# A fused two-layer kernel on one core: the mixer's skip term and its running sums are moved off GpSimd, and the residual is added ahead of y

## The chip, the cores and the metric

The kernel runs as one program on one core of a Trainium2 chip. The metric is the device time of one execution in microseconds, lower is better. A core has five engines with instruction streams of their own, which wait for each other only through semaphores: PE (TensorE, matrix products), DVE (VectorE), ACT (ScalarE), POOL (GpSimd) and SP (SyncE, which issues the DMAs).

## The reference

Two layers are applied to x (1024 tokens, 512 wide): a Mamba-2 style mixer, a SwiGLU block with 4-bit weights, a small attention and a LoRA mixture. Only the mixer is touched:

```
proj = layernorm(x) @ in_proj_w.T              # gate | hbc | dt
xBC  = silu(conv4(hbc) + conv_bias)            # x | B | C ; 64 heads of 64, 8 groups, state 128
state_t = state_{t-1} * exp(dt A) + (dt x)_t B_t ;  y_t = state_t C_t
y   = y + x * D
yn  = y * rsqrt(mean over the group's 512 columns of y*y + eps) * norm_weight * silu(gate)
x   = x + yn @ out_proj_w.T
```

## The kernel before, in words

The mixer is one pipeline over 8 groups of heads (8 heads, 512 columns each) and, inside a group, over 8 chunks of 128 tokens: 64 chunks, n = 8 g + c. Groups 1 to 6 are a hardware loop; group 0 and the last one are written out. Each engine has a fixed program order; semaphores are counted up by the engine named in their prefix. I call the chunks of a group c0 to c7.

In a chunk PE does, in this order: transposes of x into `p_x`; the products of B and C (`p_gb`); the decay exponents (L1081 into `p_in`, L1090 into the two banks `p_d0`, `p_d1`; both read as p_d in the trace); one convolution tile of the next half group (`conv_tile` "now", bank `p_tile`, three passes, L94 and L98); the output product of the chunk before (`out_product(n-1, p_d0)`, also L94 and L98, tile p_d); the state's contribution to y (L1113, `p_in`); the new state (L1121, `p_x`); in c0, c1, c4, c5 a second convolution tile ("later", bank `p_gate`); `sum_rows(n-1)`, a product with a column of ones that sums the squares of y (L1029, a column of `p_gb`); the chunk's own y (L1136, `p_y`); and a tile of gate projections (`next_gate`). `p_d0` thus holds first the decay exponents of chunk n, which ACT reads as the first em, and then the output product of chunk n-1, which DVE adds into the residual stream x_res (`residual`, L742). The decay product of chunk n+1 therefore waits for `s_res`.

DVE does the causal mask (L814), a copy of B (L815), the convolution taps (`tile_taps`: L714 over 509 to 511 columns from PSUM; L722 over 3 to 1 columns at the seam of two halves, from the SBUF tile halo), the masking of em (L826), y = p_in * e_cum (L838), the state update (L844), y += p_y (L856), the gate multiplication (L864), `residual` and `z_rest` (L734). ACT takes the exponentials (L626 em, L628 e_cum), the bias and last tap (L592), SiLU (L597, L613), the squares of y (L650), and rounds z and the weights (L602, L581, L584). POOL scales x by dt (L492, L495), decays the state (L483, `state_dec`), makes D times x (L498, `x_d`) and adds it to y (L515), folds the squares to 128 columns (L525, L528), splits weights (`w_rest` L543; `out_rest`, L551 and L554, two of the output weights in c0) and takes the power -1/2 of the variance (`norm`, L538), which `residual` needs.

The order that matters below is DVE's at the end of a chunk: y, gate multiplication, `residual`, `z_rest`; then ACT's squares, z, gate SiLU, the copy xs, a table load, em.

## Time and profile before

| | us |
|---|---|
| median of 3 runs | 1321.4 (1320.72 to 1321.72) |
| the profiled execution, its time | 1320.9 |
| its span, first to last instruction | 1319.1 |
| mixer's chunks, about | 62 to 986 of the span |
| one group of the loop | 116.4 |

PE is busy 93% of the span, DVE 72%, POOL 54%, ACT 53%. Busy PE time is the modelled end of each product, so that a product that had to wait shows as idle time ahead of its first instruction. The rows of the trace stand in a section below.

### The profile page before, as it was taken

To read this page: it belongs to the slowest core of one execution; us is meant where nothing else is said; L and a number is where in the kernel's file an instruction comes from. 1 tells how busy PE (TensorE), PEld (TensorE's weight loads), DVE (VectorE), ACT (ScalarE), POOL (GpSimd) and SP (SyncE) were. 2 spreads that over 40 slices of the span, in tenths; PEclk is the share of its full clock that TensorE was granted. 3 is DMA by queue.
4 is the path that set the end of the run, shared out by engine and by line. 5 is a ranking of instruction groups with operands and counts; after the bars stand their busy time and mean duration, and the time that the engine had idled before them with its cause. 6 is when DMAs were issued, how large, how long until landed. Compare 5 with 4: busy or idle time off the path is not lost.

```text
span 1319.1 us, 22013 instructions
## 1 busy us (share of the span) xinstructions
PE 1227.4 (93%) x6690; PEld 973.3 (74%) x6690; DVE 953.9 (72%) x1718; ACT 694.1 (53%) x1042; POOL 709.0 (54%) x739
## 2 busy tenths in 40 slices
PE   5999999999999999999999999999779999889986
PEld 4778877887777778777777877778557777667764
DVE  5786768678676866777687677769776555569995
ACT  3666675576667656665766667666333333222220
POOL 5066666666656665675566567555663444343330
PEclk9999999999999999999999999999889999999996
DMA  5111021011102101110110110010003223121200
GB/s 175 46 49 34 1 66 33 18 33 48 33 1 63 34 17 33 48 33 1 48 49 17 33 48 25 9 38 2 20 27 110 95 88 97 47 92 33 59 16 25
DMA packets 44233, 57.52 MB, mean 44 GB/s; under 512 B 10117, under 2 KB 21159, under 8 KB 43929
## 3 DMA queue, kind: packets, MB, share of 16 engines
q1 hardware_dynamic: 44185, 56.92, 14.6%
q8 instruction: 25, 0.41, 0.1%
q14 instruction: 23, 0.19, 0.1%
HBM read 49.95 MB, written 6.96 MB: 43 GB/s over the span
## 4 chain that ended last, share of the span: by engine, by line
PE 57%; DVE 19%; issue 9%; POOL 7%; ACT 5%; DMA 1%; DVEq 1%; SPq 1%; POOLq 0%; ACTq 0%
PE p_tile L94 9%; PE p_d L94 6%; DVE conv L714 6%; PE p_gate L94 5%; PE p_tile L98 4%; PE p_d L98 3%; PE p_y L1136 3%; DVE conv L722 3%; PE p_gate L98 2%; PE p_in L1113 2%; PE t_p_a L1886 2%; POOL y L515 2%; PE p_x L1121 2%; PE p_y L94 2%; PE p_d L1090 2%
## 5 line engine op out<-in xcount | busy, mean ns | idle before, releaser
L714 DVE SCALAR_TENSOR_TENSOR conv<-p_tile,conv_taps,conv 128x511 f32<-128x511 f32 x189 | 141.4, 748 | 49.2 <-ACT conv L592 34.1
L515 POOL TENSOR_TENSOR y<-y,x_d 128x512 f32<-128x512 f32 x56 | 72.2, 1288 | 129.8 <-DVE y L838 129.8
L826 DVE TENSOR_TENSOR em<-em,p_gb 128x512 f32<-128x512 f32 x128 | 82.1, 682 | 53.6 <-ACT em L626 53.5
L714 DVE SCALAR_TENSOR_TENSOR conv<-p_gate,conv_taps,conv 128x511 f32<-128x511 f32 (+2 forms) x90 | 66.9, 743 | 66.9 <-ACT conv L592 66.0
L597 ACT ACTIVATE xbc<-conv 128x512 f32<-128x512 f32 x96 | 60.7, 633 | 101.0 <-DVE conv L722 78.7
L94 PE MATMUL p_tile<-xn_hi,wc_hi 128*128 128x512 f32 x252 | 107.7, 427 | 2.3 <-ACT gate_second L613 1.4
L650 ACT ACTIVATE squares<-y 128x512 f32<-128x512 f32 x64 | 40.6, 634 | 121.1 <-DVE y L856 114.1
L94 PE MATMUL p_d<-wr_hi,zt_hi 128*128 128x512 f32 x252 | 102.5, 407 | 0.8 <-ACT em L626 0.8
L94 PE MATMUL p_d<-wr_lo,zt_hi 128*128 128x512 f32 x252 | 101.8, 404 | 0.0
L94 PE MATMUL p_tile<-xn_lo,wc_hi 128*128 128x512 f32 x252 | 98.6, 391 | 0.0
L492 POOL TENSOR_TENSOR x_w<-xs,head_g 128x512 f32<-128x512 f32 x56 | 61.6, 1101 | 55.3 <-ACT xs L622 50.3
L597 ACT ACT_TABLE_LOAD x61 | 78.3, 1283 | 5.8 <-DVE conv L722 3.2
L626 ACT ACT_TABLE_LOAD x61 | 78.3, 1283 | 1.5 <-PE p_d L1090 0.2
L543 POOL TENSOR_TENSOR wc_lo<-w_raw,wc_hi 128x512 fp32r<-128x512 f32 x48 | 61.2, 1291 | 22.8 <-ACT wc_hi L581 22.8
L626 ACT ACTIVATE em<-p_d 128x512 f32<-128x512 f32 x128 | 69.6, 596 | 5.6 <-PE p_d L1090 5.0
L495 POOL TENSOR_TENSOR x_dt<-xs,head_g 128x512 f32<-128x512 f32 x64 | 67.3, 1052 | 8.1 <-ACT xs L622 8.1
L525 POOL TENSOR_TENSOR squares<-squares 128x256 f32<-128x256 f32 x64 | 62.4, 976 | 16.8 <-ACT squares L650 16.5
L1324 POOL TENSOR_TENSOR f_w_lo<-wf,f_w_hi 128x512 fp32r<-128x512 f32 x22 | 30.4, 1380 | 72.9 <-ACT f_w_hi L1357 72.9
L98 PE MATMUL p_d<-wr_hi,zt_lo 128*128 128x512 f32 x252 | 69.2, 397 | 0.0
L1136 PE MATMUL p_y<-em,x_dt 128*64 128x128 f32 x1008 | 68.9, 279 | 0.0
L498 POOL TENSOR_TENSOR x_d<-xbc,d_g 128x512 f32<-128x512 f32 x64 | 68.2, 1066 | 0.0
L98 PE MATMUL p_tile<-xn_hi,wc_lo 128*128 128x512 f32 x252 | 67.9, 391 | 0.0
(384 smaller groups left out, 3615.3 us busy)
## 6 DMA issues: line engine op xcount, KB each, us to landing
w_raw<-w SPq DMA_DIRECT2D x108, 256.0 KB, 2.7
q_words<-q SPq DMA_DIRECT2D x33, 256.0 KB, 2.6
h_ring<-h_lo_rows SPq DMA_DIRECT2D x6, 704.0 KB, 4.8
h_lo_rows<-h_rest SPq DMA_DIRECT2D x11, 256.0 KB, 2.0
x_res<-x SPq DMA_DIRECT2D x8, 256.0 KB, 4.6
out<-out_t SPq DMA_DIRECT2D x8, 256.0 KB, 2.0
h_lo_rows<-h_rest SPq DMA_DIRECT2D x11, 128.0 KB, 1.9
gate_second<-w SPq DMA_DIRECT2D x4, 256.0 KB, 5.3
```

Source lines behind the costliest of these rows:

```text
L94: pe.matmul(out, lhs(k)[0], rhs(k)[n], start=(start and k == 0 and n == 0), stop=False)
L98: last = pe.matmul(out, lhs(k)[1], rhs(k)[0], start=False, stop=(k == k_tiles - 1))
L492: pool.tensor_tensor(by_head(x_w[:]), by_head(xs[:]), heads(DTW, c), ALU.mult)\
L495: pool.tensor_tensor(by_head(x_dt[:]), by_head(xs[:]), heads(DT, c), ALU.mult)\
L498: pool.tensor_tensor(by_tile(x_d[:]), xbc[:, 0:GW // P, c * P:(c + 1) * P], by_col(d_g[:]), ALU.mult)\
L515: pool.tensor_tensor(y[:], y[:], x_d[:], ALU.add).then_inc(s_txd, 1)
L525: pool.tensor_tensor(squares[:, 0:2 * P], squares[:, 0:2 * P], squares[:, 2 * P:4 * P], ALU.add)\
L597: act.activation(xbc[:, j, half_cols(hf)], conv[:, j % 2, :], ACT.Silu).then_inc(s_xc, 1)
L626: act.activation(em[:, c % 2, k * 512:(k + 1) * 512], p[:], ACT.Exp).then_inc(s_e, 1)
L714: ve.scalar_tensor_tensor(out=conv[:, s, sh:], in0=p[:, 0:HALF - sh], scalar=conv_w[:, bass.ds(g, 1), j, tap], in1=conv[:, s, sh:], op0=AL ...
L826: ve.tensor_tensor(m, m, gm.unsqueeze(1).broadcast_to([P, HG // 2, P]), ALU.mult)\
L1136: mm = pe.matmul(y_bank(last, c)[a:a + HD, j * P:(j + 1) * P], x_dt[:, h * HD:(h + 1) * HD], em[:, c % 2, h * P:(h + 1) * P], start=True, ...
```

## The change

1. D times x: the tile `x_d` and both POOL operations (L498, L515) are gone. DVE adds d_g[j] * xbc[:, j] in four column operations of 128x128, one for each of the 4 tiles of the group: for c > 0 in place in y behind the state update, for c0 with `p_y` as the addend in place of L861. `s_xd` is now DVE's own count.
2. The sum of squares goes into column 384 of y's bank (`p_y`) in place of `p_gb`: PE does `sum_rows(n-1)` right behind `out_product(n-1)`, DVE reads it (`variance`) behind the taps of the "now" tile, and the product L1136 into `p_y` waits for that reading (`s_v`, n).
3. `residual` stands ahead of y's last addition; in c0 DVE's split of two output weights (`w_rest`) goes ahead of it too. POOL's `norm` stands between the two `out_rest` of c0.
4. ACT rounds the four output weights of c0 ahead of that chunk's SiLU; in c0, c1, c4, c5 it takes the gate's SiLU ahead of z's rounding.
5. In the last group's chunks 4 to 7 the output product goes to `p_gate`, with no wait for em, and POOL folds the squares first; rows of the next norm (`row_rest`) go ahead of y's last addition.

The core of the diff:

```
-        return p_gate[:, 0:1] if last and CH <= c < NC else p_gb[:, 3 * P:3 * P + 1]
+        return (p_y if c < NC else p_gb)[:, 3 * P:3 * P + 1]
+    def out_bank(last, c):
+        return p_gate if last and c >= CH else p_d0
...  GpSimd
+                if last and c >= CH:
+                    sum_squares(n - 1)
-                wait(pool, s_y, n)
-                pool.tensor_tensor(by_tile(x_d[:]), xbc[:, 0:GW // P, c * P:(c + 1) * P], by_col(d_g[:]), ALU.mult)\
-                    .then_inc(s_xd, 1)
-                    for w in (OUT + 2, OUT + 3):
-                        out_rest(g, w)
+                    out_rest(g, OUT + 2)
+                if not (isinstance(g, int) and n == 0):
                     norm(n - 1, (c - 1) % 2)
-                    pool.tensor_tensor(y[:], y[:], x_d[:], ALU.add).then_inc(s_txd, 1)
+                if c == 0:
+                    out_rest(g, OUT + 3)
...  ScalarE
+                if c == 0:
+                    wait(act, s_out, n)
+                    for w in ROUNDED:
+                        w_round(g, w)
                 for tile in left + now:
                     tile_silu(*tile)
...
+                made = gate_tile(g, last, c)
+                if made and c % CH < 2:
+                    gate_silu(CH + n, made[1], made[2], gate_bank(c))
                 z_round(n, y_bank(last, c))
...  VectorE
                 for tile in now:
                     tile_taps(*tile, range(TAPPED[tile[3]]))
+                if not first:
+                    variance(n - 1, (c - 1) % 2, ss_bank(c))
...
+                if c > 0:
+                    ve.wait_ge(s_head, 4 * (g + 1))
+                    ve.wait_ge(s_t, st)
+                    for j in range(GW // P):
+                        mm = ve.scalar_tensor_tensor(out=y[:, j * P:(j + 1) * P], in0=xbc[:, j, c * P:(c + 1) * P],
+                                                     scalar=d_g[:, j:j + 1], in1=y[:, j * P:(j + 1) * P],
+                                                     op0=ALU.mult, op1=ALU.add)
+                    mm.then_inc(s_xd, 1)
+                if c == 0:
+                    for w in VE_LO:
+                        w_rest(g, w)
+                if not first and not tail:
+                    residual(n - 1, (c - 1) % NC, out_bank(last, c))
+                for k in rows_in(last, c):
+                    row_rest(k)
...
-                if not first and not tail:
-                    residual(n - 1, (c - 1) % NC)
-                for k in rows_in(last, c):
-                    row_rest(k)
...  TensorE
-                    out_product(n - 1, p_d0)
+                    out_product(n - 1, out_bank(last, c))
+                    sum_rows(n - 1, ss_bank(c))
...
                 pe.wait_ge(s_m, 2 * (n + 1))
-                if not first and not tail:
-                    sum_rows(n - 1, ss_bank(last, c))
...
-                    wait(pe, s_zlo, n)
+                    wait(pe, s_v, n)
```

Where this moves instructions, first on VectorE, chunk c0 of the loop's body. Before, from the state's copy to the two weight splits:

```order
L847 COPY state<-p_x 128x512 [waits pe_inter,ve_stu,pe_stn]
...
L714 SCALAR_TENSOR_TENSOR conv<-p_gate,conv_taps,conv 128x511
...
L729 TENSOR_SCALAR ssv<-p_gb 128x1 [waits pool_rs]
L861 TENSOR_TENSOR y<-x_d,p_y 128x512 [waits act_sq,ve_z,pool_xd,pe_intra]
...
L864 TENSOR_TENSOR p_y<-y,gate_first 128x512 [waits act_sg]
...
L742 SCALAR_TENSOR_TENSOR x_res<-p_d,g_rstd,x_res 128x512 [waits ve_res]
L734 TENSOR_TENSOR zt_lo<-p_y,zt_hi 128x512 [waits act_zhi]
...
L752 SCALAR_TENSOR_TENSOR wr_lo<-w_raw,norm_scale,wr_hi 128x512
```

The same stretch of the change:

```order
L844 COPY state<-p_x 128x512 [waits pe_inter,ve_stu,pe_stn]
...
L748 SCALAR_TENSOR_TENSOR wr_lo<-w_raw,norm_scale,wr_hi 128x512
...
L738 SCALAR_TENSOR_TENSOR x_res<-p_d,g_rstd,x_res 128x512 [waits ve_res]
...
L710 SCALAR_TENSOR_TENSOR conv<-p_gate,conv_taps,conv 128x511
...
L872 SCALAR_TENSOR_TENSOR y<-xbc,d_g,p_y 128x128 [waits ve_head]
L872 SCALAR_TENSOR_TENSOR y<-xbc,d_g,p_y 128x128 x3
...
L880 TENSOR_TENSOR p_y<-y,gate_first 128x512 [waits act_sg]
L730 TENSOR_TENSOR zt_lo<-p_y,zt_hi 128x512 [waits act_zhi]
```

The two splits and the residual now stand between the state and y. Second, VectorE in chunk c1 of the loop's body, before, from the state's part of y on:

```order
L838 TENSOR_TENSOR y<-p_in,e_cum 128x512 [waits ve_z,act_sq,pe_inter]
...
L844 TENSOR_TENSOR state<-p_x,state_dec 128x512 [waits pool_std,ve_stu,pe_stn]
...
L729 TENSOR_SCALAR ssv<-p_gb 128x1 [waits pool_rs,pe_ss]
L856 TENSOR_TENSOR y<-y,p_y 128x512 [waits pool_txd,pe_intra]
L864 TENSOR_TENSOR p_y<-y,gate_first 128x512 [waits act_sg,ve_y]
L742 SCALAR_TENSOR_TENSOR x_res<-p_d,g_rstd,x_res 128x512 [waits ve_res,pool_rs,pe_out]
```

and in the change:

```order
L725 TENSOR_SCALAR ssv<-p_y 128x1 [waits pool_rs,pe_ss]
L835 TENSOR_TENSOR y<-p_in,e_cum 128x512 [waits ve_z,act_sq,pe_inter]
...
L841 TENSOR_TENSOR state<-p_x,state_dec 128x512 [waits pool_std,ve_stu,pe_stn]
L849 SCALAR_TENSOR_TENSOR y<-xbc,d_g,y 128x128 [waits ve_t,ve_head]
L849 SCALAR_TENSOR_TENSOR y<-xbc,d_g,y 128x128 x3
L738 SCALAR_TENSOR_TENSOR x_res<-p_d,g_rstd,x_res 128x512 [waits ve_res,pool_rs,pe_out]
...
L866 TENSOR_TENSOR y<-y,p_y 128x512 [waits pool_xd,pe_intra]
L880 TENSOR_TENSOR p_y<-y,gate_first 128x512 [waits act_sg,ve_y]
```

The four column operations and the residual stand ahead of y's last addition, and the variance ahead of all. Third, TensorE around the chunk's own y, before:

```order
L1029 MATMUL p_gb<-ones_col,squares 128x1 [waits pool_sum,ve_m]
L1136 MATMUL p_y<-em,x_dt 64x128 [waits ve_zlo,pool_xdt]
```

and in the change, where the sum has gone up behind the output product:

```order
L98 MATMUL p_d<-wr_hi,zt_lo 128x512 x3
L1037 MATMUL p_y<-ones_col,squares 128x1 [waits pool_sum]
...
L1141 MATMUL p_y<-em,x_dt 64x128 [waits ve_v,pool_xdt,ve_m]
```

## Rows read from the trace of the kernel before

**Rows 1.** The page, part 1: busy time of each engine over the span

```profile
PE 1227.4 (93%) x6690; PEld 973.3 (74%) x6690; DVE 953.9 (72%) x1718; ACT 694.1 (53%) x1042; POOL 709.0 (54%) x739
```

**Rows 2.** Windows: one group of the loop; then most of the last group's end

```profile
core 0: us, PE busy (x) PEld busy (x) DVE busy (x) ACT busy (x) POOL busy (x), PEclk, DMA share, GB/s
523.90:640.30 116.40, 113.08 (x651) 90.58 (x650) 85.13 (x153) 74.65 (x110) 72.51 (x75) 1.00 0.11 32
...
935.00:987.00 52.00, 36.39 (x229) 27.93 (x230) 37.68 (x70) 15.77 (x29) 33.91 (x39) 0.86 0.10 26
```

**Rows 3.** Waits, whole span: who waited for whom, us in total, times, longest

```profile
PE p_d L1090 <- DVE x_res L742: 22.8, 22, 1.7
...
PE p_d L1090 <- DVE xn_lo L771: 6.3, 3, 2.5
PE p_gate L1029 <- POOL squares L528: 6.2, 2, 4.6
...
DVE x_res L742 <- PE p_d L98: 5.1, 3, 2.5
DVE ssv L729 <- PE p_gate L1029: 4.7, 2, 3.0
```

**Rows 4.** Timeline of PE, one group: start us, us; idle before in brackets

```profile
424.56 0.59 PE L1090 MATMUL p_d<-decay_rhs,decay_lhs 90*128 90x512 bf16 x2 [1.38 <-DVE x_res L742]
441.88 0.59 PE L1090 MATMUL p_d<-decay_rhs,decay_lhs 90*128 90x512 bf16 x2 [1.36 <-DVE x_res L742]
455.41 0.59 PE L1090 MATMUL p_d<-decay_rhs,decay_lhs 90*128 90x512 bf16 x2 [0.46 <-DVE x_res L742]
```

**Rows 5.** Timeline of DVE, same group

```profile
420.08 0.68 DVE L861 TENSOR_TENSOR y<-x_d,p_y 128x512 f32<-128x512 f32 x1
...
423.66 0.75 DVE L742 SCALAR_TENSOR_TENSOR x_res<-p_d,g_rstd,x_res 128x512 f32<-128x512 f32 x1 [1.84 <-POOL g_rstd L538]
...
428.56 3.43 DVE L722 SCALAR_TENSOR_TENSOR conv<-halo,conv_taps,conv 128x3 f32<-128x3 f32 x3
...
439.51 1.56 DVE L864 TENSOR_TENSOR p_y<-y,gate_first 128x512 f32<-128x512 f32 x1
...
510.12 0.70 DVE L864 TENSOR_TENSOR p_y<-y,gate_second 128x512 f32<-128x512 f32 x1
```

**Rows 6.** Timeline of POOL, same group

```profile
421.35 1.61 POOL L554 TENSOR_TENSOR wr_lo<-w_raw,wr_hi 128x512 fp32r<-128x512 f32 x1
...
428.45 1.04 POOL L498 TENSOR_TENSOR x_d<-xbc,d_g 128x512 f32<-128x512 f32 x1
429.47 2.52 POOL L543 TENSOR_TENSOR wc_lo<-w_raw,wc_hi 128x512 fp32r<-128x512 f32 x2
437.09 1.29 POOL L515 TENSOR_TENSOR y<-y,x_d 128x512 f32<-128x512 f32 x1 [5.10 <-DVE y L838]
...
439.48 1.04 POOL L483 TENSOR_TENSOR state_dec<-state,head_g 128x512 f32<-128x512 f32 x1
```

**Rows 7.** Source lines: duration min/median/max in ns, first and last start

```profile
L722 DVE SCALAR_TENSOR_TENSOR conv<-halo,conv_taps,conv x144: 219/222/1240, 69.7 to 927.1; 128x3 f32<-128x3 f32 x48, 128x2 f32<-128x2 f32 x48, 128x1 f32<-128x1 f32 x48
L815 DVE COPY b_tok<-p_gb x64: 269/281/292, 63.5 to 978.7; 128x128 f32<-128x128 f32 x64
```

**Rows 8.** Timeline of ACT, c2 into c3

```profile
453.36 0.63 ACT L650 ACTIVATE squares<-y 128x512 f32<-128x512 f32 x1 [2.14 <-DVE y L856]
...
457.53 1.09 ACT L626 ACTIVATE em<-p_d 128x512 f32<-128x512 f32 x2
```

**Rows 9.** Timelines of PE and DVE: own y, and state's part, in c3 and c7

```profile
463.34 1.09 PE L1136 MATMUL p_y<-em,x_dt 128*64 128x128 f32 x16
...
463.33 0.68 DVE L838 TENSOR_TENSOR y<-p_in,e_cum 128x512 f32<-128x512 f32 x1
...
519.96 1.09 PE L1136 MATMUL p_y<-em,x_dt 128*64 128x128 f32 x16
...
520.10 0.69 DVE L838 TENSOR_TENSOR y<-p_in,e_cum 128x512 f32<-128x512 f32 x1
```

More of the change, by code:

```diff
@@ L484, in group @@
                         .then_inc(s_std, 1)
-                if not (isinstance(g, int) and n == 0):
+                if not (isinstance(g, int) and n == 0) and not (last and c >= CH):
                     sum_squares(n - 1)
@@ L735, in z_rest, with residual @@
                              zt_hi[:].rearrange("p k t -> p (k t)").bitcast(F32), ALU.subtract).then_inc(s_zlo, 1)
-        def residual(m, c, p=p_d0):
+        def residual(m, c, p):
             ve.wait_ge(s_out, m + 1)
@@ L798, in group @@
         def group(g, last):
+            wait(ve, s_xdt, g * NC)
             wait(ve, s_xd, g * NC)
@@ L816, in group @@
                 for tile in left:
-                    tile_taps(*tile, range(1 if c == 1 else 2, TAPPED[tile[3]]))
-                if tail:
-                    variance(n - 1, (c - 1) % 2, ss_bank(last, c))
+                    tile_taps(*tile, range(2, TAPPED[tile[3]]))
                 for k in rows_in(last, c):
@@ L829, in group @@
                     tile_taps(*tile, range(TAPPED[tile[3]]))
+                if not first:
+                    variance(n - 1, (c - 1) % 2, ss_bank(c))
                 if tail:
-                    residual(n - 1, c - 1)
+                    residual(n - 1, c - 1, out_bank(last, c))
                     row_stats(c - 1)
@@ L854, in group @@
                 if c > 0:
-                    ve.wait_ge(s_txd, st)
+                    ve.wait_ge(s_xd, n + 1)
                     ve.tensor_tensor(y[:], y[:], p[:], ALU.add).then_inc(s_y, 1)
                 else:
-                    ve.wait_ge(s_xd, n + 1)
                     wait(ve, s_sq, n)
                     wait(ve, s_z, n)
-                    ve.tensor_tensor(y[:], x_d[:], p[:], ALU.add).then_inc(s_y, 1)
+                    ve.wait_ge(s_head, 4 * (g + 1))
+                    for j in range(GW // P):
+                        mm = ve.scalar_tensor_tensor(out=y[:, j * P:(j + 1) * P], in0=xbc[:, j, c * P:(c + 1) * P],
+                                                     scalar=d_g[:, j:j + 1], in1=p[:, j * P:(j + 1) * P],
+                                                     op0=ALU.mult, op1=ALU.add)
+                        if j == GW // P - 2:
+                            mm.then_inc(s_xd, 1)
+                    mm.then_inc(s_y, 1)
                 ve.wait_ge(s_y, n + 1)
@@ L882, in group @@
                     up.unpack(ve, 0, 1)
-                if c == 0:
-                    for w in VE_LO:
-                        w_rest(g, w)
-                else:
-                    for tile in later:
-                        tile_taps(*tile, range(1, 2))
+                for tile in later:
+                    tile_taps(*tile, range(1, 2))
         def ln_rest(c):
@@ L1071, in group @@
                 wait(pe, s_m, 2 * n)
-                wait(pe, s_v, n - 1)
                 if c % CH == 0:
@@ L1126, in group @@
                 pe.wait_ge(s_m, 2 * (n + 1))
-                if not first and not tail:
-                    sum_rows(n - 1, ss_bank(last, c))
                 pe.wait_ge(s_xdt, n + 1)
```

34 lines of the change are left out of this document (9 added, 25 removed).

## The prediction

> **What bounds the kernel now.** I read the busy shares first, then the windows, then who waits for whom, then the timeline of one group. PE is busy 93% of the span and DVE 72% [rows 1]. A group of the loop takes 116.40 us with PE busy 113.08, so a perfect change of the mixer's side work could take 3.3 us from a group, some 25 over the eight [rows 2]. The waits say where these are: 22 times, 22.8 us in all, the decay product L1090 waits for `residual` to give back bank p_d [rows 3]. In the group that I follow this is in front of c1, c2 and c3: 1.38, 1.36 and 0.46 us [rows 4]; c4 to c0 have none. The last group's second half is another matter: in 935 to 987 PE is busy 36.39 of 52 us and DVE 37.68 [rows 2], and PE waits for the next norm's rows (6.3) and for POOL's folded squares (6.2) [rows 3].
>
> Why is `residual` late? In c0 DVE has y at 420.08 + 0.68 = 420.76 but stands idle 1.84 us until POOL's `norm` comes behind four weight operations; it starts at 423.66 [rows 5], after POOL's last split, 421.35 plus 1.61 [rows 6]. In c1 it is late because DVE is: three seam operations that cost 0.222 each [rows 7] took 3.43 together [rows 5]. They end when POOL operations end: x_d 428.45 + 1.04 = 429.49, then wc_lo to 431.99 [rows 6], and 428.56 + 3.43 = 431.99. So a DVE operation with both tensors in SBUF waits out the POOL operation in progress. The gate multiplication shows the same: 1.56 beside state_dec (439.48 + 1.04), 0.70 in c6, where POOL has none to do [rows 5, 6].
>
> The Trainium skill says this in "GPSIMD Engine Reference" (table of the engine's properties): the SBUF interface is shared, with contention for DVE instructions that have two SBUF inputs or run in a 2-port mode. The trace agrees, with the 3.43 us.
>
> **Part 1, D times x on DVE.** POOL loses 1.04 and 1.29 us a chunk [rows 6]. DVE gains four operations of 128 columns. No row has this form; the nearest is the copy of 128x128 at 0.281 [rows 7]. I bound one by 0.22 below (a seam operation, of 3 columns or fewer) and by 0.35 above (0.222 plus 125 columns at the rate by which the 512 of L742 come to 0.75 [rows 5], 0.13), and take 0.27, the copy's less a little overlap: 1.1 for four, 0.9 to 1.4. "VectorE: DVE Perf Modes" of the Trainium skill (the trn2 errata) warns that small tiles pay a fixed cost each, and its formula (N + 151) / 0.96 ns for an addition gives 0.29 for N = 128, an estimate: 1.16 for four. No run here shows this form yet.
>
> The price has a second half. The columns read xbc and y, both in SBUF, directly behind the state update; POOL's state_dec is released by that very update. Before, it met the gate multiplication and cost it 0.55 to 0.86 (1.25 or 1.56 against 0.70). Now it gets in behind the first column, and the other three wait out its 1.04 [rows 6]. I take 1.0; 0 is the lower bound, if DVE keeps the access through the row of four. The gate multiplication gets its 0.55 back. From L838's start to y's end it took 0.68 + 1.29 + 0.68 and two signals of 0.1 between engines, 2.85 us; now 0.6 (L838, less overlap) + 0.6 (state) + 1.1 + 1.0 + 0.65 (`residual`, 0.75 less overlap) + 0.65 = 4.6 us, or 3.6 without the collision.
>
> **Part 2, residual early.** In c1, c2 and c3 the wait at L1090 goes: 1.38 + 1.36 + 0.46, with the pipeline's refill 1.55 + 1.53 + 0.63 = 3.7 a group at most. Cover for what it now costs ahead of y is DVE's idle time, and that is there in c4 to c7 and c0, not in c1 to c3.
>
> **Part 3, c0 in detail.** ACT's four roundings now start when the last output product is done, some 2 us sooner than before, when SiLU and its seam operations went first. POOL's first split starts with them and stands on the three seam operations of c0 that ran free of it before, at 0.222 each [rows 7]: two of them wait out 1.04 and 1.29, +1.8. Behind them come the state copy, two weight splits (both inputs in SBUF, taking turns with POOL's `norm` and second split: 2.3 for 1.3), residual 0.65, the late tap 0.65, the columns 1.1. y of c0 ends about 2.9 us later than at 420.76 [rows 5]; 1.1 is my lower bound, no collisions but ACT's later tile. Queued behind y of c0 on ACT are the squares and the gate's SiLU, and the next convolution tile waits for this SiLU since both use p_tile. That tile can start no sooner than y + 1.3, which is where it starts today. So c1: +0.3 (L1136 of c0 for the variance) - 1.55 + 1.2 (SiLU) + 0.3 (em) - 0.17 (a seam wait that goes) = +0.1.
>
> **Part 4, the variance on the way to L1136.** PE may write y's bank only after DVE has read the sum, and DVE reads it where L838 starts today. In c3 L838 starts at 463.33 and L1136 at 463.34; in c7 at 520.10 and 519.96 [rows 9]. Adding the reading (0.15) and 0.1 of signalling, PE waits 0.3 in c3 and 0.35 in c7; in c2, where two weight splits meet the seam operations, 0.5. In chunks with a later tile it costs nothing.
>
> **Part 5, the circle y to em to y.** The output product writes p_d0 and needs, as before, ACT to have read the first em from it; before, the wait at L1090 hid this. From y's end to em's start ACT takes 457.53 - 453.36 = 4.2 us [rows 8], 3.7 with a gate multiplication that is not held up. From y of c1 to y of c2 the circle is today 453.36 - 439.51 = 13.85 us [rows 5, 8]. With 4.6 for 2.85 and 0.5 back it becomes 15.1, or 14.7 where DVE has no more arrears; from L1090 to L1090 PE alone needs 455.41 - 441.88 - 0.63 = 12.9 [rows 4]. y of c1 still has about 1 us in hand. The surplus beyond it comes out as a wait of out_product for em, about 0.85 in c3 and 0.8 in c4, where the later tile ends it. Sum: c2 -1.55 + 0.5 = -1.05; c3 -0.63 + 0.3 + 0.85 = +0.5; c4 +0.8; c5 and c6 -0.2 each (SiLU ahead of z frees p_tile); c7 +0.35.
>
> A group is thus +0.1 - 1.05 + 0.5 + 0.8 - 0.4 + 0.35 = +0.3 us; 7 to 7.5 such groups, +2.2. What PE gains in c2 it gives back in c3 and c4.
>
> **Part 6, the last four chunks.** PE's waits (6.2 + 6.3) can go: the squares are folded first, the rows split earlier, no em is needed. But then DVE binds: of its 52 - 37.68 = 14.3 us idle [rows 2] I let 11.8 go (4.7 for the sum, 5.1 for the output product [rows 3], the rest in front of y), and it gains four times 1.1 and three times 1.0, 7.4. Net -4.4. Here PE's granted clock is 0.86 on average; with fewer stops it may be higher, but PE does not set the end there, so I count nothing.
>
> **Sum.** +2.2 - 4.4 = -2.2 us against the profiled execution's 1320.9, 0.5 below the median of the runs: 1319.1 expected for the median.
>
> **Rivals.**
> (a) DVE keeps up, clearly faster. For it: DVE is busy only 85.13 of 116.40, 0.8 to 1.4 a chunk more is at most 96, and POOL loses 2.3 a chunk. If consecutive columns are not interrupted (-1.0 in c1, c2, c3) and y of c0 is late by 1.1 only (-1.8), nearly all of the 3.7 come, less 0.65 of part 4: 3 a group, -22, tail -7: about 1293. Halfway, 1306. Against it: the 3.43 us row.
> (b) Slower, by one mechanism: the circle of part 5. If a column takes 0.35 and each of the four takes its turn with POOL, a circle is 0.5 to 0.8 longer in c1, c2 and c3; PE cannot give it back before c4, so a group grows by 1.5 to 2.4 instead of 0.3: 1329 to 1335. It decides from the point where the circle of c1 passes PE's own 441.88 - 424.56 - 1.55 = 15.8 us [rows 4]. For it: today c1 to c3 are already set by this circle, not by PE.
> (c) The end of the last group gives nothing, since POOL and DVE stay late: 1323.5, still within the noise.
>
> **How the numbers follow.** What a measurement of this kernel tells from no change is 0.2%, 2.6 us. My own case with its uncertainty (1314 to 1324) 0.36; (a), full or halfway, 0.32; (b) 0.24; (c) 0.08. Faster by over 0.2% is (a) and a third of my case, 0.43; within 0.2% is the rest of my case and most of (c), 0.26; slower 0.31. The range of 1302 to 1332 leaves a tenth on each side, from the fuller half of (a) and the worse half of (b).
>
> **What would show it.** Right: L1090's wait for x_res is gone (below 2 us in all); new waits of PE at L1136's successor for ssv in c2, c3, c7 and at out_product for em in c3, c4, and at c1's tile for the gate SiLU; the four columns take near 2 us together in c1 to c5 and near 1.1 in c6, c7; the seam operations of c0 take over 2 us in place of 0.73; a group takes 116 to 117.5. Wrong: a group near 113 (then no collision or a hidden one), or above 118 (then the circle is longer than I make it).

## The result and the profile after

The changed kernel took 1329.5 us (median of 4 runs, 1327.5 to 1331.9) where the kernel before took 1321.6 (4 runs, 1320.7 to 1322.5): a ratio of 1.005, 95% interval 1.0032 to 1.0068. It is 0.5% slower; 1319.1 had been forecast. The time lies inside the range given; the sign is not the one forecast.

The page of the changed kernel, its span and busy time, beside [rows 1]:

```profile
span 1325.5 us, 22030 instructions
PE 1235.9 (93%) x6690; PEld 966.6 (73%) x6690; DVE 1007.0 (76%) x1966; ACT 690.0 (52%) x1042; POOL 560.5 (42%) x619
```

D times x moved as intended: GpSimd is about 150 us less busy, VectorE about 50 us more. It is all that left GpSimd. The running sums of the title did not: the squares are still folded there, in 64 operations (L525 before, L522 after), and what moved is the bank of their row sum and its place in the order. What TensorE waits for between 60 and 940 us (total, times, longest), which answers to [rows 3]:

```profile
PE p_tile L94 <- ACT gate_second L610: 11.7, 7, 1.8
PE p_y L1141 <- DVE ssv L725: 8.0, 19, 2.2
PE p_d L94 <- ACT em L623: 2.9, 14, 0.2
PE p_tile L94 <- DVE conv L718: 1.7, 1, 1.7
```

The wait for x_res that led that list before is gone altogether. Three others took its place: for ScalarE's gate SiLU, for the variance (ssv), and for em.

Where each lies is read from the timeline of TensorE: the time from the first transposition of one chunk (L1069 before, L1077 after) to that of the next. The loop groups 1 to 6 of a kernel agree within some 0.1 us but in chunk 1, so one number stands for the six. The table has the experiments too; "low clock" counts the groups of 1 to 6 in which TensorE's granted clock falls to 1.2 GHz in chunk 1; where some have it and others not, chunk 1 is some 1.5 us longer in them, and it and the group are given for both. In group 0, which the table leaves out, e6 has it in chunk 0 and e12 in chunk 2.

| kernel | c0 | c1 | c2 | c3 | c4 | c5 | c6 | c7 | group | low clock |
|---|---|---|---|---|---|---|---|---|---|---|
| before | 14.53 | 17.34 | 14.42 | 13.48 | 15.68 | 15.84 | 13.10 | 12.00 | 116.4 | 0 |
| after | 14.95 | 17.88 / 19.35 | 13.13 | 13.92 | 16.17 | 15.71 | 12.97 | 12.44 | 117.2 / 118.7 | 3 |
| e1 | 14.96 | 17.36 | 14.36 | 13.93 | 16.16 | 15.72 | 12.97 | 12.43 | 117.9 | 0 |
| e2 | 14.60 | 21.1 to 22.7 | 13.13 | 13.92 | 16.17 | 15.71 | 12.97 | 12.44 | 120.0 to 121.6 | 6 |
| e4 | 14.96 | 17.44 | 13.79 | 13.08 | 15.71 | 15.71 | 12.97 | 12.42 | 116.1 | 0 |
| e6 | 14.96 | 17.70 | 13.14 | 13.92 | 16.17 | 15.71 | 12.97 | 12.44 | 117.0 | 0 |
| e7 | 14.96 | 17.26 | 13.79 | 13.08 | 15.71 | 15.71 | 12.97 | 12.42 | 115.9 | 0 |
| e8 | 14.96 | 17.44 | 13.13 | 13.93 | 16.17 | 15.71 | 12.97 | 12.43 | 116.7 | 0 |
| e9 | 14.62 | 18.25 / 19.70 | 12.97 | 13.59 | 16.67 | 15.71 | 12.97 | 12.10 | 116.9 / 118.3 | 2 |
| e10 | 14.62 | 17.83 / 19.26 | 12.97 | 12.97 | 15.71 | 15.71 | 12.97 | 12.11 | 114.9 / 116.3 | 5 |
| e12 | 14.54 | 17.33 to 17.89 / 19.28 | 13.05 | 13.28 | 16.15 | 15.86 | 13.12 | 12.00 | 115.3 to 115.9 / 117.3 | 1 |
| e13 | 14.62 | 17.62 | 12.97 | 12.97 | 15.71 | 15.71 | 12.97 | 12.11 | 114.7 | 0 |
| e14 | 14.62 | 18.05 / 19.63 | 12.97 | 13.59 | 16.67 | 15.71 | 12.97 | 12.10 | 116.7 / 118.3 | 3 |
| e15 | 14.62 | 16.43 | 12.97 | 12.97 | 15.71 | 15.71 | 12.97 | 12.11 | 113.5 | 0 |
| e16 | 14.62 | 16.43 | 12.97 | 13.59 | 16.67 | 15.71 | 12.97 | 12.11 | 115.1 | 0 |

The account from the starts: group 0 is 1.84 us longer than before, groups 1 to 6 together 9.0 (three by 0.8, three by 2.2), the last group up to its chunk 7 is 3.8 shorter; with 0.1 ahead of them and 0.8 won behind, that is the 6.3 us between the spans.

Most of the loss is in chunk 1. VectorE, end of chunk 0 in group 3 (start, length; before, the last three of these came ahead of any weight rest, [rows 5]):

```profile
423.15 0.15 DVE L725 TENSOR_SCALAR ssv<-p_y 128x1 f32<-128x1 f32 x1
423.33 0.69 DVE L844 COPY state<-p_x 128x512 f32<-128x512 f32 x1
423.94 3.24 DVE L748 SCALAR_TENSOR_TENSOR wr_lo<-w_raw,norm_scale,wr_hi 128x512 fp32r<-128x512 f32 x2
427.11 0.74 DVE L738 SCALAR_TENSOR_TENSOR x_res<-p_d,g_rstd,x_res 128x512 f32<-128x512 f32 x1
427.77 0.73 DVE L710 SCALAR_TENSOR_TENSOR conv<-p_gate,conv_taps,conv 128x511 f32<-128x511 f32 x1
428.43 1.11 DVE L872 SCALAR_TENSOR_TENSOR y<-xbc,d_g,p_y 128x128 f32<-128x128 f32 x4
```

ScalarE and TensorE right behind it:

```profile
429.57 0.63 ACT L644 ACTIVATE squares<-y 128x512 f32<-128x512 f32 x1 [4.76 <-DVE y L872]
430.11 0.58 ACT L610 ACTIVATE gate_second<-p_tile 128x512 f32<-128x512 f32 x1
430.58 0.59 ACT L599 ACTIVATE zt_hi<-p_y 128x512 fp32r<-128x512 f32 x1
```
```profile
430.74 0.49 PE L94 MATMUL p_tile<-xn_hi,wc_hi 128*128 128x512 f32 x1 [1.77 <-ACT gate_second L610]
431.07 0.39 PE L94 MATMUL p_tile<-xn_lo,wc_hi 128*128 128x512 f32 x1
```

Read from below: chunk 1's convolution tile wants the bank p_tile, which chunk 0's gate product still holds; its SiLU stands behind the squares of y on ScalarE, which has idled 4.76 us for y. The same stop stands in the next group, and there the matmuls behind it run slower (group 4):

```profile
547.91 0.50 PE L94 MATMUL p_tile<-xn_hi,wc_hi 128*128 128x512 f32 x1 [1.77 <-ACT gate_second L610]
548.48 0.59 PE L94 MATMUL p_tile<-xn_hi,wc_hi 128*128 128x512 f32 x1
548.86 0.63 PE L94 MATMUL p_tile<-xn_lo,wc_hi 128*128 128x512 f32 x1
549.29 0.63 PE L94 MATMUL p_tile<-xn_hi,wc_hi 128*128 128x512 f32 x1
```

A start every 0.43 us, not every 0.23. The windows of 5 us behind the stop (busy times; the clock is the number behind POOL's, 1.00 being 2.4 GHz):

```profile
312.10:317.10 5.00, 5.00 (x15) 3.94 (x16) 4.32 (x10) 3.99 (x7) 2.76 (x4) 0.66 0.04 13
430.80:435.80 5.00, 5.00 (x21) 3.91 (x22) 4.32 (x10) 4.97 (x9) 2.72 (x4) 1.00 0.02 7
547.90:552.90 5.00, 4.99 (x15) 3.99 (x16) 4.32 (x10) 3.99 (x7) 2.79 (x4) 0.66 0.02 6
```

0.66 over the window is some 3.4 us at the level of 1.2 GHz: TensorE did nothing for 1.77 us and then got the lower level in groups 2, 4 and 5, at 1.5 us each, and kept 2.4 GHz in 1, 3 and 6.

### The profile page after: what moved, and what is told of

It is laid out like the page before. It is cut to its first block and busy times, and to the rows that moved or that the text cites. A ratio compares the mean times of both kernels' runs of the same rounds, so it can differ in the third digit from the quotient of the medians.

```text
span 1325.5 us, 22030 instructions
## 1 busy us (share of the span) xinstructions
PE 1235.9 (93%) x6690; PEld 966.6 (73%) x6690; DVE 1007.0 (76%) x1966; ACT 690.0 (52%) x1042; POOL 560.5 (42%) x619
## 3 DMA queue, kind: packets, MB, share of 16 engines
q1 hardware_dynamic: 44185, 56.92, 14.4%
## 5 line engine op out<-in xcount | busy, mean ns | idle before, releaser
L522 POOL TENSOR_TENSOR squares<-squares 128x256 f32<-128x256 f32 x64 | 47.1, 737 | 208.2 <-ACT squares L644 208.1
L94 PE MATMUL p_tile<-xn_hi,wc_hi 128*128 128x512 f32 x252 | 111.4, 442 | 12.6 <-ACT gate_second L610 11.7
L94 PE MATMUL p_d<-wr_hi,zt_hi 128*128 128x512 f32 x236 | 95.2, 403 | 3.0 <-ACT em L623 2.9
L730 DVE TENSOR_TENSOR zt_lo<-p_y,zt_hi 128x512 fp32r<-128x512 f32 x63 | 43.6, 692 | 69.9 <-ACT zt_hi L599 69.9
L94 PE MATMUL p_d<-wr_lo,zt_hi 128*128 128x512 f32 x236 | 93.2, 395 | 0.0
L498 POOL TENSOR_TENSOR x_w<-xs,head_g 128x512 f32<-128x512 f32 x56 | 59.1, 1055 | 79.5 <-ACT xs L619 61.3
L849 DVE SCALAR_TENSOR_TENSOR y<-xbc,d_g,y 128x128 f32<-128x128 f32 x224 | 91.0, 467 | 0.9
L1141 PEld LDWEIGHTS p_y<-em,x_dt 128*64 128x64 f32 x1008 | 54.5, 136 | 40.9 <-issue 40.8
L94 PEld LDWEIGHTS p_tile<-xn_hi,wc_hi 128*128 128x128 f32 x252 | 47.9, 190 | 31.6 <-ACT gate_second L610 15.1
```

The lines of the kernel that those rows point to most:

```text
L94: pe.matmul(out, lhs(k)[0], rhs(k)[n], start=(start and k == 0 and n == 0), stop=False)
L498: pool.tensor_tensor(by_head(x_w[:]), by_head(xs[:]), heads(DTW, c), ALU.mult)\
L522: pool.tensor_tensor(squares[:, 0:2 * P], squares[:, 0:2 * P], squares[:, 2 * P:4 * P], ALU.add)\
L849: mm = ve.scalar_tensor_tensor(out=y[:, j * P:(j + 1) * P], in0=xbc[:, j, c * P:(c + 1) * P], scalar=d_g[:, j:j + 1], in1=y[:, j * P:(j + ...
L1141: mm = pe.matmul(y_bank(last, c)[a:a + HD, j * P:(j + 1) * P], x_dt[:, h * HD:(h + 1) * HD], em[:, c % 2, h * P:(h + 1) * P], start=True, ...
```

## The experiments

Ratios are to the kernel before, run beside each, with the 95% interval. Three theories at the start: A, y of chunk 0 is late because VectorE's weight rests stand ahead of it; B, the column operations lengthen every circle of y; C, instruction fetch at the head of VectorE's loop.

**e1: the weight rests back at the chunk's end.**

```diff
-                if c == 0:
-                    for w in VE_LO:
-                        w_rest(g, w)
                 if not first and not tail:
                     residual(n - 1, (c - 1) % NC, out_bank(last, c))
...
                 for tile in later:
                     tile_taps(*tile, range(1, 2))
+                if c == 0:
+                    for w in VE_LO:
+                        w_rest(g, w)
```

> The changed kernel with one piece undone: VectorE's two weight rests of chunk 0 (L748, 3.24 us beside GpSimd's) stand at the end of the chunk again and no more ahead of the residual and y. Theory A, y of chunk 0 late: the stop of 1.77 us in front of the convolution tile of chunk 1 (waiting for ScalarE's gate SiLU, which waits for y) falls below 0.3 us in every group, the stretch of chunk 1 loses the 0.5 us (groups 1, 3, 6) or 2.0 us (groups 2, 4, 5) that it had over before, no half clock is seen behind it; 7 x 0.5 + 3 x 1.5 = 8 us less, 1320 to 1323 us. Theory B, the four column operations make every circle of y longer and the weight rests only lie in it: the stop stays over 1.2 us and the time stays at 1328 to 1330. Theory C, instruction fetch at VectorE's loop start: the 2.4 us idle at the loop start stays, and so does the time.

1333.3 us, 1.0078 (1.006 to 1.0095): not better than the changed kernel. A was right about the stop and wrong about the time. The stop for the gate SiLU in chunk 1 is gone and no low clock follows, but the rests are now late themselves, in front of the product in chunk 1:

```profile
433.14 0.47 PE L94 MATMUL p_d<-wr_hi,zt_hi 128*128 128x512 f32 x1 [0.90 <-DVE wr_lo L748]
```

From there the delay goes on: 0.45 us for ssv in chunk 1, then 0.49 for the gate SiLU and 0.42 for ssv in chunk 2, which is 1.2 us longer. In the kernel before the rests stood at the same place in the order and were no earlier by much (they end 4.6 us into chunk 1, here 4.9), but there the product starts 5.7 us into the chunk, behind the 1.38 us for x_res, and here it could start at some 4.2.

**e2: the same, with ScalarE's roundings and GpSimd's two rests of chunk 0 as before.**

```diff
-                if c == 0:
-                    wait(act, s_out, n)
-                    for w in ROUNDED:
-                        w_round(g, w)
                 for tile in left + now:
                     tile_silu(*tile)
+                if c == 0:
+                    wait(act, s_out, n)
+                    w_round(g, ROUNDED[0])
+                    w_round(g, ROUNDED[1])
                 for T, tg, j, _ in later:
                     tile_in(T, tg, j)
+                if c == 0:
+                    w_round(g, ROUNDED[2])
+                    w_round(g, ROUNDED[3])
...
```

> As the run before, and ScalarE's four weight roundings of chunk 0 and GpSimd's two norm-weight rests also stand as in the kernel before (roundings behind the tile's SiLU, both rests ahead of the rstd power). Theory A: no more than the piece on VectorE matters, 1320 to 1323 us, within 1 us of the run before. Theory B: 1328 to 1330. If ScalarE's order matters by itself (the roundings ahead of the SiLU hold up the tile that chunk 0 needs), this run is 1 to 3 us below the run before.

1351.9 us, 1.022 (1.0202 to 1.0239). All expectations missed. Chunk 0 falls to 14.6 us, but GpSimd's rests now end late, the residual's rstd power stands behind them, and chunk 1 has two stops (1.0 to 1.8 us for x_res, then 2.15 for the gate SiLU) and the lower clock in every group. The order change on ScalarE and GpSimd belongs to the earlier residual. In group 0, which has no residual to wait for in its chunk 0, that chunk takes 12.63 us as before and not 14.4.

**e3: 100 VectorE memsets of one column ahead of the first group**, in its idle time, so that the loop's code lies elsewhere.

```diff
+        for i in range(40):
+            ve.memset(own_pad[:, i:i + 1], 0.0)
         for c in range(NC + 3):
...
+            for i in (range(40, 75), range(75, 100))[a]:
+                ve.memset(own_pad[:, i:i + 1], 0.0)
             ve.wait_ge(dt_mm, a + 1)
```

> The changed kernel with 100 tiny VectorE memsets of one column put into its idle time ahead of the first group (they move the loop's code by 100 instructions, and leave the loop itself alone). Theory C, instruction fetch: the loop of VectorE (346 instructions) now lies in other blocks; the idle time of 2.4 to 2.7 us in front of the head table copies at the start of groups 2 to 6 vanishes, and the two instruction packets there too. If that idle time is what stops TensorE in chunk 1, the time falls by 3 to 8 us, to 1321 to 1326; if it is covered (group 1, which has no such idle time, is as long as groups 3 and 6), the time stays within 0.7 us of 1329.5. Theories A and B: 1328.8 to 1330.2.

1331.2 us, 1.0061 (1.0047 to 1.0075): as the changed kernel. The idle time at the loop's head is all there, so the place of the code doesn't make it, and its price stayed open until e11.

**e4: D times x on GpSimd again**, the rest as changed.

```diff
+                wait(pool, s_y, n)
+                pool.tensor_tensor(by_tile(x_d[:]), xbc[:, 0:GW // P, c * P:(c + 1) * P], by_col(d_g[:]), ALU.mult)\
+                    .then_inc(s_xd, 1)
...
                 if c == 0:
                     out_rest(g, OUT + 3)
+                if c > 0:
+                    pool.wait_ge(s_t, st)
+                    pool.wait_ge(s_xd, n + 1)
+                    pool.tensor_tensor(y[:], y[:], x_d[:], ALU.add).then_inc(s_txd, 1)
...
```

> The changed kernel with D times x on GpSimd again (the product x_d behind x_dt, and its addition to y behind the rstd power), everything else as changed. Theory B, the column operations are the loss: chunks 2 to 7 of a group fall back to before or below, the time goes under 1318 us. Theory A: y of chunk 0 is still late (weight rests ahead of it, and GpSimd has more to do beside them): the stop in chunk 1 stays over 1.2 us, and GpSimd's addition behind the residual's power comes late in chunks 1 to 7: 1326 to 1336 us. VectorE's loop has its old length of 315 instructions, so by theory C its idle time at the loop start is gone in this run.

1317.2 us, 0.9954 (0.994 to 0.9968): B's number, faster than before. The waits of TensorE in it:

```profile
PE p_y L1134 <- DVE ssv L732: 10.3, 20, 2.2
PE p_tile L94 <- ACT gate_second L617: 8.6, 7, 1.3
```

As A said, the stop in chunk 1 stays over 1.2 us, at 1.33; but no group has the lower clock behind it. Chunks 3 and 4 are 0.85 and 0.46 us shorter, chunk 2 is 0.66 longer.

**e5: the kernel before with the new order of the last four chunks alone.**

```diff
-        return p_gate[:, 0:1] if last and CH <= c < NC else p_gb[:, 3 * P:3 * P + 1]
+        return (p_y if last and CH <= c < NC else p_gb)[:, 3 * P:3 * P + 1]
...
+                if last and c >= CH:
+                    sum_squares(n - 1)
...
-                    out_product(n - 1, p_d0)
+                    out_product(n - 1, out_bank(last, c))
+                if tail:
+                    sum_rows(n - 1, ss_bank(last, c))
...
```

> The kernel before with the change in the last four chunks alone (sum of squares ahead of GpSimd's other work, in y's bank; residual into the gate bank, its product ahead of the row sum); D times x, the residual and the weights of all other chunks as before. The changed kernel gained 4.4 us there against before by the starts of its chunks. If that part stands by itself: 4 to 5 us under the kernel before, ratio 0.9965 to 0.997. If the gain there came from GpSimd having no D times x: within 1 us of before.

1319.7 us, 0.9971 (0.9961 to 0.9981), 3.8 us: most of the gain stands by itself. By the starts of the last group's chunks 4 to 7 it is 3.4 us here and 4.75 in the changed kernel.

**e6 and e7: chunk 0's gate SiLU ahead of the squares**, with the columns on VectorE and with D times x on GpSimd.

```diff
+                made = gate_tile(g, last, c)
+                if c == 0:
+                    gate_silu(CH + n, made[1], made[2], gate_bank(c))
                 act.wait_ge(s_y, n + 1)
...
```

> The changed kernel with ScalarE's gate SiLU of chunk 0 ahead of its squares of y (in the kernel before and in the changed one it stands behind them). Theory D: y of chunk 0 is late, the gate SiLU stands behind its squares, and so the convolution tile of chunk 1 finds its bank taken for 1.77 us; after such a stop TensorE in some groups runs at half clock for 3.4 us (1.45 us lost each). Here the gate SiLU can run 1.5 us before the bank is wanted: the stop goes to 0, chunk 1 falls from 17.9 or 19.35 us to 16.1 to 17, no half clock behind it; 7 to 14 us less, 1316 to 1322. Rival: y of chunk 1 is the next thing to be late by as much (its circle starts with y of chunk 0), chunk 1 or 2 gives the 1.77 us back and the time stays above 1326, or only the half clocks go (about 1325).

> The changed kernel with D times x on GpSimd again and the gate SiLU of chunk 0 first. By theory D the stop of 1.33 us per group that stayed in the run with D times x on GpSimd goes as well (no half clock was there): 5 to 9 us below that run's 1317.2, 1308 to 1313. Rival: given back in chunks 1 and 2, 1316 to 1318.

e6: 1326.2 us, 1.0019 (1.001 to 1.0029); e7: 1317.9, 0.9959 (0.9944 to 0.9974), as e4. The stop for the SiLU is gone and the rival took place: the product behind the tile waits for em, 1.73 us in e6 and 1.3 in e7, and chunk 1 keeps all but 0.2 us. What e6 won is the lower clock, absent from its six groups of the loop (group 0 has it, in chunk 0).

**e8: only chunk 0's D times x back on GpSimd**, added in one operation.

```diff
-                    for j in range(GW // P):
-                        mm = ve.scalar_tensor_tensor(out=y[:, j * P:(j + 1) * P], in0=xbc[:, j, c * P:(c + 1) * P],
...
+                    ve.tensor_tensor(y[:], x_d[:], p[:], ALU.add).then_inc(s_y, 1)
...
```

> The changed kernel with D times x of chunk 0 alone made by GpSimd and added by one whole-width VectorE addition (0.67 us in place of four column operations in 1.11), the column operations of chunks 1 to 7 as changed. Theory E: in chunk 0 the columns cost 0.44 us, and the stop of TensorE behind them grows from 1.33 to 1.77 us, over the length at which half clock follows it. Then the stop is 1.3 us, no half clock is seen, 7 x 0.44 + 4.4 = 7.5 us less, 1321 to 1323. Rival: it is GpSimd's state decay beside the columns in chunks 1 to 5 that costs nearly all; then 1327 to 1330.

1322.8 us, 0.9994 (0.9985 to 1.0004), as theory E said: 7 us of the loss hang on 0.44 us of VectorE's work, some 4.4 of them by the lower clock in three groups. Chunk 1 is 17.44 us in all six groups.

**e9 and e10: the row sum of the loop's chunks in a column of p_d1**, so that the y product waits for no variance; with and without the columns on VectorE.

```diff
-        return (p_y if c < NC else p_gb)[:, 3 * P:3 * P + 1]
+        if last or c == NC:
+            return (p_y if CH <= c < NC else p_d1 if c < CH else p_gb)[:, 3 * P:3 * P + 1]
+        return p_d1[:, 3 * P:3 * P + 1]
...
+                    if not tail:
+                        pe.wait_ge(s_e, 2 * (n + 1))
                     sum_rows(n - 1, ss_bank(c, last))
...
-                    wait(pe, s_v, n)
+                    wait(pe, s_v if tail else s_zlo, n)
```

> The changed kernel with the sum of squares of all chunks but the last four in a column of the decay bank p_d1 (free between ScalarE's second exp and the next chunk's decay product) in place of y's bank, so that the product for y waits for no variance. Theory F: each wait of the y product for VectorE's ssv (0.26, 0.28 and 0.43 us in chunks 7, 0 and 3) costs itself and 0.15 us of restart (the chunks 0 and 7 are 0.42 and 0.44 us longer than before); without them a group is 0.4 + 0.6 + 0.4 = 1.4 us shorter, the time 7 to 10 us less, 1319 to 1322. Rival: y's circle is what is late and takes the time back in the next chunk; then chunks 0 and 7 are shorter, chunks 1 and 4 longer, and the time stays over 1326.

> The same with D times x on GpSimd again (that kernel, with the row sum in y's bank, took 1317.2). There the waits for ssv are 0.24, 0.28 and 0.75 us (chunks 7, 0 and 2). Theory F: 1.7 us less per group, 1305 to 1309. Rival: y's circle takes it back, 1313 to 1317.

e9: 1326.6 us, 1.0022 (1.001 to 1.0033); e10: 1316.0, 0.9947 (0.9932 to 0.9962), both short of theory F. The chunks with the wait did get shorter (in e9 c0, c3 and c7 by 0.33), but TensorE comes to the unchanged stop in chunk 1 the earlier: 2.13 us in e9, 1.69 in e10. In e9 chunk 4 also takes back 0.5, with a wait for em of 0.70 us in place of 0.21. And e10 loses its gain to the clock (two of its groups, first one without and then one with it):

```profile
426.50:431.50 5.00, 5.00 (x25) 3.99 (x24) 4.81 (x10) 4.97 (x8) 3.97 (x5) 1.00 0.00 0
541.00:546.00 5.00, 5.00 (x17) 3.94 (x16) 4.64 (x11) 4.08 (x7) 3.04 (x3) 0.66 0.00 0
```

**e11: e4 with four tiny memsets a chunk**, which make VectorE's loop 347 instructions long in place of 315 (346 in the changed kernel), not counting the waits that stand as instructions of their own.

```diff
+                for i in range(4):
+                    ve.memset(own_pad[:, 4 * c + i:4 * c + i + 1], 0.0)
                 z_rest(n, p)
```

> The changed kernel with D times x on GpSimd (1317.2 us), and four tiny VectorE memsets of one column per chunk in front of the gated rest, where VectorE waits about 1 us for ScalarE in any case. They make VectorE's loop as long as in the changed kernel (347 instructions in place of 315; it had 346 there) and do no work. Instruction fetch by length: the idle time of 2.4 us at the start of groups 2 to 6 and the two instruction packets come back. If that idle time costs nothing (chunk 1 of group 1, which has none, was as long as in groups 3 and 6), the time stays within 1 us of the run without memsets; if it is a part of the loss, the time is 3 to 12 us longer. If the fetch hangs on the place of the code and not on its length, no idle time is seen.

1318.8 us, 0.9967 (0.9955 to 0.998); the intervals of e4 and e11 overlap, and a group is 116.1 us in both. The idle time of 2.5 us at the loop's head came back in groups 2 to 6: it follows the length of the loop, and costs nothing here. Theory C is out as a cause.

**e12: the kernel before with D times x on VectorE and nothing else** (the four column operations as changed).

```diff
+                    for j in range(GW // P):
+                        mm = ve.scalar_tensor_tensor(out=y[:, j * P:(j + 1) * P], in0=xbc[:, j, c * P:(c + 1) * P],
+                                                     scalar=d_g[:, j:j + 1], in1=y[:, j * P:(j + 1) * P],
+                                                     op0=ALU.mult, op1=ALU.add)
+                    mm.then_inc(s_xd, 1)
...
```

> The kernel before with D times x on VectorE (the four column operations, as in the changed kernel) and nothing else changed. In the changed kernel taking the columns out gained 1.1 us per group and three half clocks, 12 us in all. Theory G, the columns lengthen y's circle wherever they stand: 0.5 to 1.5 us more per group, 1325 to 1332. Rival: in the kernel before GpSimd's addition, which stood in the circle, costs as much as the columns (1.14 us, and the wait for GpSimd goes): chunks 2 to 6 as before, 1319 to 1324.

1321.7 us, 0.999 (0.9979 to 1.0): the rival. Alone, the columns cost nothing (a loop group is mostly 0.5 to 1.1 us shorter; group 4 is 0.9 longer and group 0 2.5, each with one stretch at the lower clock): B is out too, as a theory of the columns by themselves.

**e13 and e14: e10 and e9 with the gate SiLU first** (the edits above together).

> D times x on GpSimd, the row sum in p_d1's column, and the gate SiLU of chunk 0 first. With the row sum there and the SiLU last, chunks 0, 2, 3 and 7 were 0.3 to 0.8 us shorter, but chunk 1 took 19.26 us in five of six groups (17.83 in the sixth), at half clock behind a stop of 1.7 us: the gain was lost there. If it is the stop behind the gate SiLU that brings the half clock (theory D), then with the SiLU first chunk 1 is 17.3 to 17.7 us in every group, a group 114.3 to 114.8, and the time 1303 to 1307. Rival: the stop only moves to the wait for ScalarE's em (1.3 to 1.8 us in the two runs with the SiLU first) and, grown by the earlier start, brings the half clock as well: 1313 to 1317.

> The changed kernel with its columns on VectorE, the row sum in p_d1's column and the gate SiLU of chunk 0 first. Theory D: no half clock, chunk 1 at 17.9 to 18.2 us (18.25 with the SiLU last), a group 116.6: 1322 to 1325. If the wait for em is as long as the stop was (over 1.7 us) and brings half clock: 1326 to 1331.

e13: 1309.3 us, 0.9895 (0.9879 to 0.9912), groups 0 to 6 without the lower clock, though its stop, now for em, is 1.66 us. e14: 1326.8, 1.0019 (1.0008 to 1.003), with a stop of 2.09 us for em and the lower clock in three groups. So it is not this SiLU that brings it.

**e15 and e16: the weight rests between the gated y and its rest**, where VectorE waits for ScalarE anyway; there ScalarE's order is squares, z rounding, SiLU; row sum in p_d1. e15 has D times x on GpSimd, e16 the columns as changed.

```diff
-                if c == 0:
-                    for w in VE_LO:
-                        w_rest(g, w)
                 if not first and not tail:
                     residual(n - 1, (c - 1) % NC, out_bank(last, c))
...
+                if c == 0:
+                    for w in VE_LO:
+                        w_rest(g, w)
...
```

> D times x on GpSimd, the row sum in p_d1's column, and VectorE's two weight rests of chunk 0 behind the gated y in front of its rest (where VectorE waits for ScalarE), with ScalarE's order there squares, z rounding, gate SiLU. Theory A in its mended form (the place of the weight rests makes y of chunk 0 late by 3.2 us, and at the chunk's end they are late themselves, 0.9 us for the product in chunk 1): here neither is late, no stop and no half clock in chunk 1, which takes 15.9 to 16.6 us; a group 113 to 114, the time 1295 to 1302. Rival: the next circle (em, then y of chunk 1) takes it back in chunks 1 and 2: 1303 to 1310.

> The same with the columns on VectorE, as changed. Theory A in its mended form: no stop in chunk 1, no half clock, and the columns of chunk 0 are off the path; what they still cost in chunks 3 and 4 is 0.6 to 1 us a group: 1300 to 1308. If the columns alone were the loss, 1318 or more.

e15: 1300.4 us, 0.9832 (0.9817 to 0.9846), the fastest here. e16: 1312.3, 0.9913 (0.9899 to 0.9927), 1.4% faster than the changed kernel by the two ratios. VectorE in e15 (group 3 begins at 401.32):

```profile
413.05 0.75 DVE L747 SCALAR_TENSOR_TENSOR x_res<-p_d,g_rstd,x_res 128x512 f32<-128x512 f32 x1
414.74 0.68 DVE L869 TENSOR_TENSOR y<-x_d,p_y 128x512 f32<-128x512 f32 x1
416.70 2.07 DVE L757 SCALAR_TENSOR_TENSOR wr_lo<-w_raw,norm_scale,wr_hi 128x512 fp32r<-128x512 f32 x2
```

y of chunk 0 begins 13.4 us into the group, not 16.0. The rests take 2.07 us, not 3.24, since GpSimd's are over by then (its last ends at 415.2). TensorE in the same chunk 1:

```profile
417.96 0.50 PE L94 MATMUL p_tile<-xn_hi,wc_hi 128*128 128x512 f32 x1 [0.43 <-ACT gate_second L619]
```

## Why the prediction was wrong

**The step that failed** is the sum for chunks 0 and 1, "+0.1" a group; measured it is +0.42 in chunk 0 and +0.54 or +2.0 in chunk 1, so 1.0 or 2.4. Of the two terms of the whole, the groups' +2.2 us came out as +11.8 (1.84 in group 0, 9.0 in groups 1 to 6, 0.9 in the last group's first four chunks) and the end's −4.4 as −5.5 (4.75 by the start of the last chunk, 0.8 behind it).

- The stop for the gate SiLU was put at 1.2 us, with 0.3 for em behind it. It is 1.77, em has no wait of its own there, and the stop costs 2.0 us: the second product of that tile starts 3.69 us into the chunk, and 1.67 in e1, which has no such stop. Against that stand the 1.55 us taken away, as forecast. The stop is long because y of chunk 0 ends 17.1 us into the group, where before it ended at 13.3: 3.8 us later and not 2.9. The prediction had VectorE's rests at 2.3 us; beside GpSimd's own rests they take 3.24. And the columns end y 0.44 us later than one whole-width addition, which the prediction had counted; without that the stop is 1.33 (e4 and e8).
- Chunk 0's +0.42 was put at 0.3. The wait for ssv is 0.28 us, as forecast, and costs 0.33 (e9, without it, has 14.62 for 14.95); the other 0.08 is there in e9 too, and was in no term.
- The clock behind the stop was in no term: 1.5 us in three of six groups, 4.4 us in this execution. Which groups have it is not fixed by the stop: they are 2, 4 and 5 here and 2, 3 and 5 in e3, and the three other runs of the changed kernel have a mean clock of 0.974 where this one has 0.976, and are 1.7 to 4.4 us longer. The median stop of [rows 4], 1.38 us, had never brought it. e8, with a stop of 1.33 and no lower clock, is back at the kernel before.
- The last group's chunk 2 has a wait of 2.2 us for ssv, the longest in the list above, where 0.5 was forecast; with the row sum in p_d1 (e9) it is gone, but 1.5 us for em come in the chunk behind it.
- Group 0 was counted like the others. It grew by 1.84 us, its chunk 0 alone by 1.77, with the one wait for conv in the list above. VectorE's three seam operations of three columns and less take 3.07 us there:

```profile
69.71 3.07 DVE L718 SCALAR_TENSOR_TENSOR conv<-halo,conv_taps,conv 128x3 f32<-128x3 f32 x3
```

while GpSimd makes the rests whose roundings the change moved forward:

```profile
69.14 1.30 POOL L551 TENSOR_TENSOR wr_lo<-w_raw,wr_hi 128x512 fp32r<-128x512 f32 x1
70.38 1.05 POOL L548 TENSOR_TENSOR w_raw<-w_raw,norm_scale 128x512 f32<-128x512 f32 x1
71.51 1.26 POOL L551 TENSOR_TENSOR wr_lo<-w_raw,wr_hi 128x512 fp32r<-128x512 f32 x1
```

The seam row of [rows 5] showed such a pairing at 3.43 us, and the prediction used it for chunk 0 of the loop (2.21 us in place of 0.74, +1.8 forecast, +1.5 measured); for group 0 it made no term. e2, with the roundings and rests where they were, has 0.73 us there and chunk 0 as before.

**The steps that held.** Chunk 2: −1.05 forecast, −1.3 measured; chunk 3: +0.5, +0.44; chunk 4: +0.8, +0.5; chunks 5 and 6: −0.2 each, −0.13; chunk 7: +0.35, +0.44; the last four chunks: −4.4, and −4.75 by the start of the last one (e5 −3.4). The pitch of a column operation was put at 0.27 us: four take 1.14 us with GpSimd idle, and 1.92 in chunks 1 to 5 beside the state decay.

Some of these numbers held better than their terms. The waits for em in chunks 3 and 4 were put at 0.85 and 0.8 us and are 0.21 each; the wait for ssv is 0.43 in chunk 3, not 0.3, and missing from the loop's chunk 2, where 0.5 was forecast. At the end 6.2 us for the folded squares went, but of the 6.3 for the next norm's rows 5.8 stayed, and waits of 3.4 us for the state and 3.7 for z's rounding are new. That these sums came out near is in part luck.

**The rivals.** The longer circle of y, the rival priced at 1329 to 1335, gave the measured number, and e4 seems to prove it. It is half true, and the number is luck: it has chunks 1 to 3 grow by the circle, and what grew most is chunk 1, by the stop and the clock behind it, while chunk 2 got shorter. e16 against e15, which differ in nothing but the columns, shows what these cost once the rests are out of the way: chunk 3 +0.62, chunk 4 +0.96 us, 1.6 a group, 0.8% in all. e12 shows that in the old order they cost nothing. In the changed kernel the rest of the change gains 0.5% (e4) and the columns lose 1.0% on top. The greater part of that, 0.56% by e8, goes through chunk 0 alone, where the rests had made y late already: e16, with every column on VectorE, the rests behind the gated y and the row sum in p_d1, is faster than before. That the rests' place makes the stop is shown by e1, where it alone is changed and the stop goes. What the place is worth in time is read from e16 against e9, which differ in it and in ScalarE's order of two operations beside it: stop 2.13 to 0.44 us, chunk 1 by 1.8 us shorter, 1.1% in time. What part of that the order on ScalarE has was not tried apart.

**What stays open** is what decides on the lower clock. Among the kernels here, no group has it behind a stop of 0.4 to 1.4 us (before, e1, e4, e7, e8, e11, e15, e16). Longer stops are mixed: for the SiLU 1.69 us 5 of 6 (e10), 1.77 us 3 of 6 (after, and e3), 2.13 us 2 of 6 (e9); for em 1.66 and 1.73 us none of 6 (e13, e6), 2.09 us 3 of 6 (e14); for x_res, 1.6 to 2.1 us, 1 of 6 (e12; the longest two without it); for the SiLU 2.15 us close behind 1.0 to 1.8 for x_res, 6 of 6 (e2). In group 0, 14 of these kernels stop for 1.7 us in chunk 0, and only e6 has the lower clock behind it. The length alone doesn't order them; e2 says that what stood still just before may count too, which no run here tried by itself.

## What to carry to other kernels

Price a moved operation where it lands: what runs beside it there, and who has waited behind the thing it now stands ahead of; with the same two rests a few operations later the kernel is some 14 us faster (e16 against e9, with ScalarE's order beside it). A stop that one engine's slack hides today has a length that the next edit uncovers, so after each gain look for the stop that TensorE now reaches earlier. And undo a change one part at a time from both ends: part on its own, and all but the part; here one part changed the time by nothing alone, the rest by −0.5%, and both together by +0.5%.
